# A graph network on one core: all zeros of the query array stored ahead of the first table

## The reference

```python
h = jnp.maximum(_layernorm(x, axis=-1), 0.0)
k = typed_linear(h, Wk, ntype)      # also q and v, by the type of the node
kw = typed_head_linear(k[src], rel_att, etype)
qw = typed_head_linear(q[dst], rel_att, etype)
a = (kw * qw).sum(-1) * rel_pri[:, etype].T / sqrt_d
m = typed_head_linear(v[src], rel_msg, etype)
...
```

## Time and profile before

| what | us |
| --- | --- |
| median of three runs | 11756.29 |
| the profiled execution's own time | 11757.73 |
| its span, first to last instruction | 11755.6 |
| end of GpSimd's last scatter in the first stage | 376.06 |
| first instruction of the next stage | 389.06 |

### The profile page before, as it was taken

The page is one execution under the profiler, slowest core; times in us unless marked ns, Lnnn a source line. Parts: engine busy times, 40 slices in busy tenths (PEclk is TensorE's granted clock), DMA queues, the critical chain, the costliest instruction groups (busy, mean ns, idle before and its releaser), DMA issues. The chain is left out here.

```text
span 11755.6 us, 88443 instructions
## 1 busy us (share of the span) xinstructions
PE 1335.8 (11%) x6735; PEld 1000.0 (9%) x6735; DVE 4012.2 (34%) x5478; ACT 3490.3 (30%) x4561; POOL 8127.3 (69%) x8534
## 2 busy tenths in 40 slices
PE   6100000030000000496111000200000010000001
PEld 4100000020000000374000000200000010000001
DVE  3365555645555555696111111111111101111111
ACT  3333333312222222375333222223222212332221
POOL 5777777677777776401777777677777767777776
PEclk8555555555555555798555555555555555555555
DMA  9333333323333333000222222222222212222222
GB/s 348 129 112 108 108 108 111 105 39 102 110 110 107 113 107 81 13 1 23 67 65 66 65 68 62 62 51 56 53 56 56 53 50 51 56 53 56 56 53 50
DMA packets 448676, 922.38 MB, mean 78 GB/s; under 512 B 211206, under 2 KB 241837, under 8 KB 432952
## 3 DMA queue, kind: packets, MB, share of 16 engines
q0 software_dynamic: 272736, 378.88, 14.7%
q1 hardware_dynamic: 157672, 535.74, 12.5%
q10 hardware_dynamic: 17648, 2.29, 0.1%
HBM read 456.45 MB, written 459.77 MB: 78 GB/s over the span
## 5 line engine op out<-in xcount | busy, mean ns | idle before, releaser
L912 POOL DMA_INDIRECT arena<-tab,src x6087 | 5746.2, 944 | 2631.0 <-issue 1890.5
L2334 DVE TENSOR_TENSOR_SCAN arena<-cv_keep,arena 128x768 f32<-128x768 f32 (+1 forms) x476 | 751.9, 1627 | 5040.6 <-ACT arena L2190 5040.6
L912 POOL DMA_INDIRECT arena<-tab,spread x1539 | 1453.1, 944 | 469.3 <-issue 469.0
L2179 ACT COPY cv_keep<-keep 128x736 f32<-128x736 f32 x204 | 166.0, 814 | 2707.6 <-issue 2707.6
L2195 ACT COPY arena<-arena 128x1472 f32<-128x1472 f32 (+1 forms) x204 | 588.2, 2883 | 551.6 <-DVE arena L2334 551.6
L2190 ACT COPY arena<-arena 128x1472 f32<-128x1472 f32 x204 | 545.2, 2673 | 666.4 <-DMA arena<-tab,src 430.0
L1147 PE MATMUL e_t<-ident,arena 128*68 128x128 f32 (+1 forms) x2 | 0.8, 396 | 4037.2 <-PEq L1492 2046.4
L2258 PE MATMUL cv_t<-ident,arena 128*81 128x128 f32 (+1 forms) x294 | 137.9, 469 | 2616.8 <-ACT arena L2202 1722.9
L1147 PEld LDWEIGHTS e_t<-ident,arena 128*68 128x68 f32 (+1 forms) x2 | 0.3, 132 | 4037.6 <-issue 4037.6
L2272 PE MATMUL cv_t<-ident,arena 128*64 128x128 f32 (+1 forms) x3 | 1.3, 426 | 2975.7 <-ACT arena L2195 2975.7
L1835 PE MATMUL po_u<-arena,Hn 128*128 128x448 bf16 x1564 | 300.9, 354 | 279.9 <-DVE Hn L1942 279.9
(11 more groups left out here) (373 smaller groups left out, 6810.2 us busy)
## 6 DMA issues: line engine op xcount, KB each, us to landing
arena<-tab SPq DMA_DIRECT2D x11520, 0.2 KB
arena<-tab ACTq DMA_DIRECT2D x6912, 0.2 KB
rows<-arena SPq DMA_DIRECT2D x68, 1506.5 KB, 5.6
rows3b<-arena SPq DMA_DIRECT2D x136, 736.0 KB
arena<-tab,src POOLq DMA_INDIRECT x6087
rows<-arena SPq DMA_DIRECT2D x68, 920.0 KB
rows<-arena SPq DMA_DIRECT2D x68, 828.0 KB, 4.5
arena<-tab SPq DMA_DIRECT2D x3200, 0.5 KB
```

What stands on the lines that cost most here:

```text
L912: pool.indirect_dma_start(out=rows[b][:, j, :], out_offset=None, in_=table, in_offset=bass.IndirectOffsetOnAxis(ap=idx[:, at:at + 1].bitca ...
L2334: ins = v.tensor_tensor_scan(out=part, data0=keep[:, 0:(f1 - f0) * C1], data1=part, initial=0.0, op0=ALU.mult, op1=ALU.add)
```

## The change

The zero stores of all 64 pieces are issued ahead of the loop over the tables, and the loop has none. The constants AHEAD and FILLED go. Nothing else differs.

```diff
-    AHEAD = 16
-    FILLED = (BLANKS - AHEAD) // GROUP
-    assert AHEAD + FILLED * GROUP == BLANKS and FILLED < MIDDLE + 2
...
-            for n in range(0, AHEAD, 2):
+            for n in range(0, BLANKS, 2):
                 blank(slice(n, n + 2))
 
-            def body(i, n, filling=False):
+            def body(i, n):
                 for x in range(n // 2):
                     wait(sp, s_tca, i * PER + (x + 1))
                     sp.dma_start(tab[sl(i, GROUP, 2 * x, 2), :, :].rearrange("a p n -> p a n"),
                                  tb[x % 2].rearrange("p a e c -> p a (e c)")).then_inc(s_st[x % 2], 16)
-                    if filling:
-                        blank(sl(i, GROUP, AHEAD + 2 * x, 2))
                 wait(sp, s_q, i * PER + n // 2)
                 sp.dma_start(q_tab[:, sl(i, GROUP, 0, n), :], q[:, sl(i, GROUP, 0, n), :]).then_inc(s_qdone, 16)
 
-            body(0, GROUP, filling=True)
-            with sp.Fori(1, FILLED) as i:
-                body(i, GROUP, filling=True)
-            with sp.Fori(FILLED, MIDDLE + 2) as i:
+            body(0, GROUP)
+            with sp.Fori(1, MIDDLE + 2) as i:
                 body(i, GROUP)
```

## The result

The changed kernel takes **11783.33 us**, the median of 12 runs (11780.37 to 11788.23), against 11757.71 us for 12 runs of the kernel before (11754.08 to 11767.40): a ratio of 1.0022, 95% interval 1.0013 to 1.0031, so **25.6 us slower**. In the profiled executions the next stage starts at 416.58 instead of 389.06 us, 27.5 us later; what is behind it took 11366.5 us before and 11368.2 after, no more apart than two executions of one kernel. The forecast was 11775 us, 18.7 us above the 11756.29 from which it started: the measured time lies inside the range and on the forecast side, with a loss larger by a third than forecast. The 0.2% that the prediction had put as the border of what counts as no change lies inside the interval, so whether the loss is past it stays unsettled.

The account below looks back on a forecast made before the run. Zeros landing last were taken to gate GpSimd's scatters, and after the change VectorE's indices: 16.1 + 2.9 = +19.0 us, next stage at 408.1 instead of 389.06, forecast 11775 us, range 11764 to 11788.

Parts of the forecast that it names:

- step 3: VectorE's start indices, behind the sixth group mask: ready at 260.5 us, releasing the first scatter at 260.6, 16.1 us later.
- Step 1: First table's landing behind the zeros: 39.7 MB at 412 GB/s take 96.3 us, so table copy 3 starts at 174.2.
- the slow bound of 101.3: Time for the 39.7 MB at 392 GB/s, the slowest 10 us with a full queue: 101.3 us, +5.0.
- Rival A: Zero stream slower than the mixed one, deciding from 393 GB/s downward: slower by over 0.2%, 11780 at 392; chance 0.15.
- Step 2: Table copies 3 to 7: copy 6 at 188.8, then an unchanged 16.76 us through root and normalization, copy 7 at 205.5.
- Step 4: GpSimd's 98 scatter steps: six VectorE group masks fall among them instead of four, +2.9 us.
- Step 5: The tables' own end: SyncE done at 394.5 us, GpSimd's last scatter ending at 395.1, so GpSimd last by little.
- rival B: The tables end the stage: at a pace of 4.5 us instead of 4.26, near +27 us, 11783; chance 0.07.
- Rival C: SyncE's queue doesn't hold the first table back, which lands 6 us after issue: about +1 us, 11757; chance 0.05.
- D: The changed kernel is faster, only through an unseen effect in later stages; chance 0.03.

Follow-up runs that it names:

- the first experiment: The changed kernel with VectorE's computation of the start indices moved ahead of the end of the second normalization: 11777.37 us, ratio 1.0014 to the kernel before.
- the table of pieces ahead: The kernel before with 24, 32, 40 pieces of zeros ahead instead of 16: ratios 0.9991, 0.9985, 0.9997; with ScalarE's root early, 16, 24, 32, 64: 0.9996, 0.9988, 0.9982, 1.0011.
- The late gathers: The changed kernel with GpSimd's gathers of windows held back until all zeros have landed: 11832.78 us in one run.

## Why the prediction was right, and where it was off

**The mechanism held.** The loss comes from step 3: the work that gives the indices hangs on the tables, the tables wait for the zeros, and from then on the indices release the scatters. The release (0.3 us behind VectorE's L835), the first experiment and the table of pieces ahead show it.

**Step 1 was the term that was mis-sized most.** Its 39.7 MB at 412 GB/s gave 96.3 us and copy 3 at 174.2; it took 101.6 and came at 179.45, 5.3 us later, just beyond the slow bound of 101.3. I had taken the 40 us that were "nearly all zeros" as nearest in kind. The late gathers show what it lacked: the gathers beside the stream take its rate down (402 GB/s on the mean of 60 to 160 us, 415 without them), and half of the parts land six microseconds late, for which the copy waits. Counting bytes over a rate that is a mean over 16 engines leaves that tail out. Rival A named this place and direction; in no stretch read before 172 us was the mean rate below the 393 GB/s from which it was to decide, but 39.7 MB in 101.6 us are 391. Its sign, a copy 3 well after 180, was just not met.

The page that I weighed here (the Trainium skill, "DMA: Bandwidth & Descriptors", section "Bandwidth") has the 358 GB/s, read whole, as what each core gets when both cores of the HBM domain stream, and puts a core alone above it. This kernel runs on one core, and the 415 GB/s over 80 us agree with that; 358 was no bound to weigh here. No run here has a second core streaming.

**Step 2 was short by 3 us.** From copy 6 to copy 7 I had kept 16.76 us; it took 19.21. TensorE's timeline, the eight matmuls of pairs 4 and 7 in the changed kernel:

```profile
181.65 3.78 PE L625 MATMUL fp_tab<-Wrel,arena 64*128 64x512 f32 x8 [119.56 <-ACT arena L542]
...
209.90 3.79 PE L625 MATMUL fp_tab<-Wrel,arena 64*128 64x512 f32 x8
```

and the latter's counterpart in the kernel before, after a standstill of 13.7 us:

```profile
112.89 1.99 PE L632 MATMUL fp_tab<-Wrel,arena 64*128 64x512 f32 x8
```

Pair 4 took 3.78 as foreseen. That pair 7 would run slow as well, 3.79 instead of 1.99, I had not: I took the chain as free of DMA waits, and so of the same length, and left TensorE's clock out of it. That part was chance either way: with the gathers late, the same matmuls took 1.99 us (see the last section). Another 0.6 us lie between copies 4 and 5 (4.81 instead of 4.24).

**Step 3** was right in itself: mask 6 stood 0.72 us behind copy 17 (0.76), the computation took 9.2, the scatter followed after 0.3. The zeros ended 67 us sooner than before, not some 75.

**Step 4** was right: six long scatters, 134.2 us in place of 130.6, 3.6 against 2.9. The inference on the Trainium skill's page "SBUF — State Buffer", section "SBUF: two separate sides", against which I had set the rows would have given nought; the rows were the better guide. The same section also says that a VectorE operation with two SBUF inputs does hold a GpSimd instruction that reads SBUF, and the six long scatters, which take their rows and indices from there, agree with that.

**Step 5** had the right end (SyncE's last wait to 403.2, 8.7 later than forecast for the reasons of steps 1 and 2) but a wrong margin. I compared it with the end of the last scatter instruction; GpSimd is through 9.4 us later (1.2 to the landing, 8.2 behind it), so the margin was 10.3 us. That also puts rival B further away than I had it.

The sum: 5.3 (step 1) + 3.1 (step 2, with 0.1 from the ten copies of step 3) + 0.7 (step 4) - 0.6 (the stage's end, 12.4 instead of 13.0) = 8.5 us over the forecast of 408.1, which gives the 416.6 measured. Nearly all of it lies on one side, so the forecast did not come inside the range by errors that cancel. Rival C (the queue doesn't hold the table back) is out: copy 3 came 25.8 us after the first table's issue, 24.0 before. D didn't occur.

## What to carry to other kernels

When a transfer that one consumer waits for is moved ahead, list what it is moved past and follow that to its own last consumer: where both feed the same instruction, the best place is where the two arrive together (here 32 pieces ahead, between the 16 of the kernel before and the 64 of the change), and the way there can be read off in two columns, when each condition is met. The pieces were tried in steps of eight, so the best place is known no more finely than that. A stall that the move creates can be used: work that hangs on neither transfer belongs under it. And a transfer has landed only when the last of its 16 parts has, so a small stream of gathers beside a large one costs its consumers more than its share of the bytes.

## What was not expected of the hardware

With GpSimd's gathers beside it (128 rows of 128 bytes each 1.25 us, 82 gathers or 1.34 MB from 60 to 170 us) a stream of zero stores ran at 402 instead of 415 GB/s, and the first store behind it landed 10.8 us later than without them, of which the missing bytes (99 gathers, 1.6 MB) are some 4 us. At its end the engines were busy for 0.55 of 6 us, while eight of the 16 parts of the first table had landed and eight had not. TensorE's eight matmuls of pair 7 were slow (3.79 us) after 11.07 us without work in the changed kernel and fast (1.99) after 13.73 us without work in the kernel before. The granted clock agrees: 0.51 is the lower of its two levels (1.2 GHz), 0.74 a rise to the upper one (2.4 GHz) within the stretch. The busy time of the stretch, PE first and the granted clock third from the end, in the changed kernel and then in the kernel before:

```profile
205.00:214.00 9.00, 8.45 (x30) 5.81 (x31) 7.81 (x14) 1.40 (x4) 0.00 (x0) 0.51 0.00 0
```

```profile
109.00:115.00 6.00, 5.80 (x30) 4.51 (x31) 6.00 (x6) 1.20 (x4) 4.88 (x4) 0.74 0.69 266
```

The long standstill ahead of it isn't the reason. With the gathers late, TensorE had stood still for 108 us and worked for 12 when a gap of 11.08 us came, as in the changed kernel, and yet the matmuls of pair 7 were fast (the granted clock is 0.75 from 194 to 203 us):

```profile
198.55 1.99 PE L626 MATMUL fp_tab<-Wrel,arena 64*128 64x512 f32 x8
```

And with 24 and 32 pieces ahead, where TensorE had no standstill of that length, they were slow (3.79) behind gaps of 12.20 and 13.07 us. So neither the length of the gap nor a long standstill before it tells these runs apart, and what does stays open; in an estimate these 1.8 us are a term that may fall either way. The row of the changed kernel from 205 to 214 us shows the DMA engines with nothing to do for these 9 us, which the kernel before filled in part with zeros. In the nine runs in which GpSimd ended the stage and that have SyncE waiting for it, 8.2 to 8.3 us lie between the landing of its last scatter and the end of that wait. Where SyncE is last, the next stage starts 3.2 us behind its last landing.
